# Softmax weights of the first two batches turned in fp32 by TensorE and normalised after P x V

## The reference

```
q, kv  = ln(x), ln(ctx)
qp, kp, vp = q @ Wq.T + bq, kv @ Wk.T + bk, kv @ Wv.T + bv
scores = qh @ kh.T / sqrt(32) - scale[h] * dist(query, key) + offset[h]
attn   = softmax(scores)                  # over the 256 keys
x      = x + (attn @ vh) @ Wo.T + bo
x      = x + gelu(ln(x) @ W1.T + b1) @ W2.T + b2
```

## Time and profile before

| | |
|---|---|
| Runs | 1235.98, 1234.48, 1235.89 us, median 1235.89 |
| Profiled execution | span 1232.5 us from the first to the last instruction; no time of its own around it is given |
| PE | 1203.1 us busy (98%), 9288 products |
| VectorE | 948.1 us busy (77%) |
| ScalarE | 878.1 us busy (71%) |
| GpSimd | 968.8 us busy (79%) |
| Chain that ended last | PE 85%, POOL 4%, DVE 4%, ACT 3%, issue 2% |

### The profile page before, as it was taken

The page is one execution under the profiler, slowest core; times in us unless marked ns, Lnnn a source line. Parts: engine busy times, 40 slices in busy tenths (PEclk is TensorE's granted clock), DMA queues, the critical chain, the costliest instruction groups (busy, mean ns, idle before and its releaser), DMA issues.

```text
span 1232.5 us, 27315 instructions
## 1 busy us (share of the span) xinstructions
PE 1203.1 (98%) x9288; PEld 784.8 (64%) x9288; DVE 948.1 (77%) x2525; ACT 878.1 (71%) x2036; POOL 968.8 (79%) x1191
## 2 busy tenths in 40 slices
PE   8898889999999999999999999999999999999998
PEld 3444466666666666666666666666666666666664
DVE  5899988879897878898787879888787878667321
ACT  7899787777767786777767686777767676676231
POOL 5687989889797879889797878889797878767410
PEclk8999999999999999999999999999999999999999
DMA  8599999988889898988989897998889897787433
GB/s 253 168 236 219 249 211 195 212 195 206 191 199 206 195 218 186 208 205 201 199 190 211 199 220 182 214 201 193 204 189 208 200 212 172 163 180 174 137 118 120
DMA packets 469179, 241.60 MB, mean 196 GB/s; under 512 B 384672, under 2 KB 409392, under 8 KB 469040
## 3 DMA queue, kind: packets, MB, share of 16 engines
q1 hardware_dynamic: 469040, 239.86, 83.7%
HBM read 109.66 MB, written 12.58 MB: 99 GB/s over the span
## 4 chain that ended last, share of the span: by engine, by line
PE 85%; POOL 4%; DVE 4%; ACT 3%; issue 2%; DMA 1%; SPq 1%; DVEq 0%; POOLq 0%; ACTq 0%
PE ps_down L696 27%; PE ps_up L681 27%; PE ps_qk L616 11%; PE ps_vo L640 6%; PE ps_vo L637 6%; PE ps_s L652 4%; PE ps_pv L666 4%; POOL soft L1335 1%; POOL soft L1352 1%; DMA xT<-x_nat 1%; DVE soft L1139 1%; ACT soft L849 1%; DVE p_nat L1157 0%; DVE p_nat L1153 0%; DVE w L1083 0%
## 5 line engine op out<-in xcount | busy, mean ns | idle before, releaser
L681 PE MATMUL ps_up<-hT,w 128*128 128x256 f16 x3072 | 377.2, 273 | 1.6 <-ACT u L895 1.6
L696 PE MATMUL ps_down<-w,hid 128*128 128x512 f16 x1536 | 372.9, 379 | 1.5 <-DMA w<-x_scratch 1.1
L1344 POOL TENSOR_SCALAR p_nat<-soft,row_inv 128x256 f16<-128x256 f32 x468 | 300.2, 652 | 78.9 <-DVE row_inv L1147 78.6
L681 PEld LDWEIGHTS ps_up<-hT,w 128*128 128x128 f16 x3072 | 300.4, 98 | 90.6 <-ACT u L895 1.9
L849 ACT ACTIVATE soft<-soft,neg_max 128x256 f32<-128x256 f32 x512 | 255.3, 500 | 115.7 <-DVE neg_max L1139 114.5
L1139 DVE CUSTOM_DVE_ANT_0 soft<-ps_s,soft,factor 128x256 f32<-128x256 f32 x512 | 225.6, 477 | 126.5 <-PE ps_s L652 126.3
L1157 DVE SCALAR_TENSOR_TENSOR p_nat<-soft,row_inv,p_nat 128x256 f16<-128x256 f32 x468 | 268.1, 612 | 1.9 <-POOL p_nat L1344 1.9
L1352 POOL TENSOR_SCALAR soft<-dist,scale_neg,offset 128x512 f32<-128x512 f32 x256 | 234.2, 915 | 12.6 <-DVE p_nat L1157 10.0
L895 ACT ACTIVATE u<-ps_up,bias,up_scale 128x256 f32<-128x256 f32 x256 | 142.7, 557 | 133.3 <-PE ps_up L681 131.9
L696 PEld LDWEIGHTS ps_down<-w,hid 128*128 128x128 f16 x1536 | 148.6, 97 | 133.2 <-DMA w<-x_scratch 1.8
L1360 POOL TENSOR_SCALAR hid<-u,hid_scale 128x1024 f16<-128x1024 f32 x64 | 81.2, 1268 | 110.6 <-ACT u L901 110.6
(11 more groups left out here) (135 smaller groups left out, 1565.2 us busy)
## 6 DMA issues: line engine op xcount, KB each, us to landing
w<-x_scratch SPq DMA_DIRECT2D x256, 256.0 KB, 3.0
stack<-qk_parts SPq DMA_DIRECT2D x256, 96.0 KB
raw<-in_ctx SPq DMA_DIRECT2D x32, 256.0 KB, 3.8
raw<-in_x SPq DMA_DIRECT2D x32, 256.0 KB, 3.0
c_stage<-in_w SPq DMA_DIRECT2D x16, 512.0 KB, 4.7
x<-in_x SPq DMA_DIRECT2D x32, 256.0 KB, 4.2
out<-x SPq DMA_DIRECT2D x32, 256.0 KB, 3.3
tok_rows<-in_tok_xy SPq DMA_DIRECT2D x16, 256.0 KB, 3.9
```

Source lines behind the costliest of these rows:

```text
L681: mm = e.matmul(ps_up[s % 2][:, 0:L], w_1_sb[:, wp, k, m * P:(m + 1) * P], hT[:, b % 2, :, xp * KT + k, :], start=(k, wp, xp) == (0, 0, 0) ...
L696: mm = e.matmul(ps_down[tt][:], hid[:, chunk % HID_RING, i, hp, tt * P:(tt + 1) * P], w_2_sb[:, s % W2_RING, wp, :], start=(m == 0 and (hp ...
L1344: mine = e.tensor_scalar(p_nat[:, nat, HI, lc, :], soft[:, ring, lc, :], row_inv[:, ring, lc:lc + 1], 1.0, ALU.mult, ALU.mult)
```

## The change

For items 0 to 31 (batches 0 and 1, `FIRST` = 32) the weights stay unnormalised fp32 and are not split.

- ScalarE's `exps` has no row sum; `scaled_sums`, `inverse`, `p_normalise`, `p_hi`, `p_hi_odd`, `p_lo` and `p_turn` are not done for these items.
- PE's `turn(i)`, in slot i + 3 right behind the scores: four fp32 transposes of 128x128, with `soft` as the stationary operand and an identity as the moving one, into `ps_down[i % 2]`. ScalarE's `whole(i)`, in slot i + 4 before `exps`, copies the bank of 512 columns into `pT_whole`, which lies where `pT` lies.
- The values of batches 0 and 1 are kept in fp32 (`v_whole`), one copy of ScalarE and no `v_lo`.
- PE's `attend_whole(G)`, in slot 9 + 4G: eight fp32 products of 256 columns for P x V into `ps_pv[:, 0:256]`, and eight with a stationary of ones for the row sums into `ps_pv[:, 256:512]`.
- VectorE's `attn_whole(G)`, in slot 10 + 4G behind `score_max`: a reciprocal of 128x256 from PSUM into `attn_n`, and a product of 128x256. ScalarE's `attn_hi` and VectorE's `attn_lo` then read `attn_n`.
- `keep_busy` counts two steps for a turn and eight for a group in place of three, writes to `ps_down`, and waits for `whole(slot - 4)`. The output bias is formed in `ps_pv` in place of `ps_down[0]`.
- GpSimd builds the identity (a memset and an `affine_select` of 128x128) before its first slot; `bias_tile` waits for `s_turn` where it waited for `s_plo`.

The core of the diff, each hunk where the functions above are:

```diff
+pT_whole = sb("pT_whole", [P, PT_RING, TC, L], F32, at["pT"])
+v_whole = sb("v_whole", [P, 2, TC, D], F32, at["v_parts"])
+ident = sb("ident", [P, P], F32, at["p_nat"] + (NAT_RING - 1) * 2 * LC * T * 2)
...
-ALL, FIRST = 20, 32
...
+FIRST = 2 * H
+FIRST_HG = FIRST // HPG
+FIRST_TILES = 2 * LC
+SPLIT = N_ITEMS - FIRST
...
-        for i in due(slot, 4, ITEM, N_ITEMS):
-            p_turn(i)
+        for i in due(slot, 4 + FIRST, ITEM, SPLIT):
+            p_turn(FIRST + i)
...
+    def turn(i):
+        ring = i % SOFT_RING
+        gate.wait_ge(s_id, ID_EYE)
+        gate.wait_ge(s_row, ROW_V)
+        gate.wait_ge(s_exp, 2 * i + 2)
+        gate.wait_ge(s_whole, i - 1)
+        for tc in range(TC):
+            for lc in range(LC):
+                at_col = tc * L + lc * P
+                mm = e.transpose(ps_down[i % 2][:, at_col:at_col + P], soft[:, ring, lc, tc * P:(tc + 1) * P], ident[:])
+        mm.then_inc(s_turn)
+
+    def attend_whole(G):
+        b, hg = divmod(G, HG)
+        gate.wait_ge(s_whole, HPG * G + HPG)
+        gate.wait_ge(s_vhi, n_half(b, 1))
+        gate.wait_ge(s_bo_all, 1)
+        gate.wait_ge(s_an, G)
+        for tc in range(TC):
+            for j in range(HPG):
+                h = hg * HPG + j
+                e.matmul(ps_pv[32 * j:32 * j + 32, 0:L], v_whole[:, b, tc, h * HD:(h + 1) * HD],
+                         pT_whole[:, (4 * G + j) % PT_RING, tc, :], start=(tc == 0), stop=(tc == TC - 1))
+        for tc in range(TC):
+            for j in range(HPG):
+                mm = e.matmul(ps_pv[32 * j:32 * j + 32, L:2 * L], one[:].to_broadcast([P, HD]),
+                              pT_whole[:, (4 * G + j) % PT_RING, tc, :], start=(tc == 0), stop=(tc == TC - 1))
+        mm.then_inc(s_pv)
...
+        for i in due(slot, 3, ITEM, FIRST):
+            turn(i)
...
-            taken = 1 + (3 if due(slot, 9, GROUP, N_HG) else 0) + (6 if slot % 2 else 0) + (6 if slot >= UP else 0)
+            taken = 1 + (2 if due(slot, 3, ITEM, FIRST) else 0) + (8 if due(slot, 9, GROUP, N_HG) else 0) + (6 if slot % 2 else 0) + (6 if slot >= UP else 0)
             taken += vo_done + (4 if due(slot, 1, ITEM, MT) else 0)
             taken += 16 if slot == 4 else 0
-            keep_busy(ps_pv if slot < 9 else ps_down[0], max(0, SLOT_STEPS - taken))
+            if slot < 2:
+                keep_busy(ps_pv, max(0, SLOT_STEPS - taken))
+            else:
+                gate.wait_ge(s_row, ROW_V)
+                gate.wait_ge(s_whole, min(slot - 3, FIRST))
+                keep_busy(ps_down[slot % 2], max(0, SLOT_STEPS - taken))
...
+        if b < 2:
+            e.activation(v_whole[:, b, tt, :], ps_vo[:], ACT.Copy).then_inc(s_vhi)
+            return
...
+        if i < FIRST:
+            for lc in range(LC):
+                gate.wait_ge(s_max, 2 * i + lc + 1)
+                e.activation(soft[:, ring, lc, :], soft[:, ring, lc, :], ACT.Exp, scale=-1.0,
+                             bias=neg_max[:, ring, lc:lc + 1]).then_inc(s_exp)
+            return
...
+    def whole(i):
+        gate.wait_ge(s_turn, i + 1)
+        gate.wait_ge(s_pv, (i - PT_RING) // 4 + 1)
+        e.activation(pT_whole[:, i % PT_RING, :, :].rearrange("p c l -> p (c l)"), ps_down[i % 2][:], ACT.Copy).then_inc(s_whole)
...
+        gate.wait_ge(s_o, n_half(b - 2, 1))
+        if G < FIRST_HG:
+            gate.wait_ge(s_an, G + 1)
+            e.activation(attnT[:, b % 2, HI, hg, :], attn_n[:], ACT.Copy).then_inc(s_ahi)
+            return
...
-        for i in due(slot, 3, ITEM, N_ITEMS):
-            if by_scalar(i):
-                p_hi_odd(i)
+        for i in due(slot, 4, ITEM, FIRST):
+            whole(i)
...
+    def attn_whole(G):
+        gate.wait_ge(s_pv, G + 1)
+        gate.wait_ge(s_alo, G)
+        e.reciprocal(attn_n[:], ps_pv[:, L:2 * L]).then_inc(s_recip)
+        gate.wait_ge(s_recip, G + 1)
+        e.tensor_tensor(attn_n[:], ps_pv[:, 0:L], attn_n[:], ALU.mult).then_inc(s_an)
...
+            e.tensor_tensor(attnT[:, b % 2, LO, hg, :], attn_n[:], attnT[:, b % 2, HI, hg, :], ALU.subtract).then_inc(s_alo)
...
             score_max(i)
-        for k in due(slot, 2, 2, N_ITEMS // 2):
-            inverse(k)
+        for k in due(slot, 2 + FIRST, 2, SPLIT // 2):
+            inverse(FIRST // 2 + k)
+        for G in due(slot, 10, GROUP, FIRST_HG):
+            attn_whole(G)
...
+            p_lo(FIRST + i)
...
-        gate.wait_ge(s_plo, i - SOFT_RING + 1)
+        gate.wait_ge(s_turn, min(i - SOFT_RING + 1, FIRST))
+        gate.wait_ge(s_plo, n_split(i - SOFT_RING))
...
+    e.memset(ident[:], 1.0).then_inc(s_id)
+    gate.wait_ge(s_id, ID_EYE - 1)
+    e.affine_select(ident[:], ident[:], pattern=[[-1, P]], compare_op=ALU.is_equal, fill=0.0, base=0, channel_multiplier=1).then_inc(s_id)
...
+            p_hi(FIRST + i)
```

More of the change, by code:

```diff
@@ L120, in build_block @@
         bias_1 = sb("bias_1", [P, MT], F32)
+        attn_n = sb("attn_n", [P, L], F32)
         b_o_sb = sb("b_o", [P, D], F32)
@@ L186, in build_block, with n_split, n_pair_split @@
         N_CHUNKS = MT // CH
-        ALL, FIRST = 20, 32
[L191 to L200, removed]
+        FIRST = 2 * H
+        FIRST_HG = FIRST // HPG
+        FIRST_TILES = 2 * LC
+        SPLIT = N_ITEMS - FIRST
+        def n_split(i):
+            return i - FIRST + 1
+        def n_pair_split(k):
+            return k - FIRST // 2 + 1
         UP = 31
@@ L292, in vo_empty @@
             kind, b, n = vo_before[use]
-            return {"v": (s_vlo, n_half(b, n)), "o": (s_x1, n_half(b, n))}[kind]
+            if kind == "o":
+                return s_x1, n_half(b, n)
+            return v_ready(b, n)
         x_rows = x.rearrange("b (c p) d -> (b c) p d", p=P)
@@ L575, in value_bias_out @@
                 for k in range(KT):
-                    mm = e.matmul(ps_down[0][:], bias_v[:, k, :], w_stage[SEC_O][:, k, :], start=(k == 0), stop=(k == KT - 1))
+                    mm = e.matmul(ps_pv[:], bias_v[:, k, :], w_stage[SEC_O][:, k, :], start=(k == 0), stop=(k == KT - 1))
                 mm.then_inc(s_brow_o)
@@ L1062, in bias_out @@
                 gate.wait_ge(s_bo, DMA)
-                e.tensor_tensor(b_o_sb[:], ps_down[0][:], b_o_sb[:], ALU.add).then_inc(s_bo_all)
+                e.tensor_tensor(b_o_sb[:], ps_pv[:], b_o_sb[:], ALU.add).then_inc(s_bo_all)
             def bias1_columns():
@@ L1241, in vector_program @@
                         mlp_out(2 * b + tt)
-                for i in due(slot, 3, ITEM, N_ITEMS):
-                    if not by_scalar(i):
-                        p_lo(i)
+                for i in due(slot, 3 + FIRST, ITEM, SPLIT):
+                    p_lo(FIRST + i)
                 for which in range(2):
@@ L1277, in vector_program @@
                     for b in due(slot, V_PROJ[tt] + 2, BATCH, B):
-                        v_lo(b, tt)
+                        if b >= 2:
+                            v_lo(b, tt)
         def gpsimd_program(engine):
@@ L1400, in gpsimd_program @@
                     bias_tile(i)
-                for i in due(slot, 2, ITEM, N_ITEMS):
-                    if by_scalar(i):
-                        p_normalise(i)
-                    else:
-                        p_hi(i)
+                for i in due(slot, 2 + FIRST, ITEM, SPLIT):
+                    p_hi(FIRST + i)
                 for w in range(AT_W1, N_W):
```

58 lines of the change are left out of this document (24 added, 34 removed).

## The result

| | before | after |
|---|---|---|
| median (range), 4 runs each | 1235.93 (1234.48 to 1238.63) us | 1250.24 (1249.44 to 1253.47) us |
| ratio, 95% interval | | 1.0122 [1.011, 1.0135], slower |
| profiled execution, span | 1232.5 us | 1251.7 us |
| start of slot 9 / 31 / 37 on PE | 74.56 / 159.61 / 183.85 us | 75.12 / 176.25 / 203.16 us |

The change costs 14.3 us; 1256 was forecast, within 1238 to 1280. The profiled execution of after is the slowest of its four runs (the spans of the other three are 1247.7 to 1248.5), so the two traces differ by 19.2 us, some 3 of which are its own.

What follows compares the result with a forecast made beforehand. PE and VectorE hold each other before slot 37, PE sets the pace after; +15.5 us (slots 9 to 31), +3 (slot 34), +1.5 (slot 37), 0 (slots 2 to 8) make +20, span 1252.5, timed 1256 us, range 1238 to 1280.

Steps and rivals of the forecast that it cites:

- Five pairs of slots between go by PE, 6.92: Slots 11 and 12 and the like: PE sets the pace, 3.23 + 3.69 = 6.92 us each, 34.6 together.
- Product end 4.9 / 5.3 / 4.0: PE's start of slot 9+4G to the products' end: 4.9 us; 5.3 in slots 17, 21, 25; 4.0 in 29.
- The rest of VectorE's slot 2.6: VectorE's other work in slots 10+4G after the pair, less what is removed: 2.6 us for all six.
- A group of fp32 products 1.9: PE's P x V group, 16 products of 256 columns with four column groups side by side: 1.9 us.
- Case C: PE pays more: fp32 halves hold up the next column group or turns cost 0.88 us; 1270 us, chance 10%.
- Reciprocal 2.1: VectorE's 128x256 reciprocal, once per group: 2.1 us, extrapolated from the medians of one and four columns.
- Six times slots 9 and 10: Slots 9 and 10 of six groups, 2 x 10.95 + 3 x 11.35 + 10.05 us: 66.0 together.
- Slots 31 to 37 +3: Slot 34: ScalarE's `attn_hi` waits for the pair, 2.55 and 1.06 us more product time, less slack: +3 us.
- PE's waits for `neg_max`: Sign: `ps_s` waits grow from 11.8 to over 20 us, one of 2 to 3 us every fourth slot.
- Case B: The clock falls in PE's new pauses, +3 us for each of up to seven groups: 1277 us, chance 20%.
- D: The reciprocal on VectorE is cheap, 0.41 us, 13.6 us less: 1242 us, 1235 to 1248, chance 13%.
- E: The chain fits: cheap reciprocal, products and turns; six groups win 3.6 us, nothing added later: 1232 us, chance 12%.

Runs made afterwards that it cites:

- e12: e8 with `attn_whole` again right behind `score_max`; late `attn_hi`/`attn_lo` and nine places kept: 1249.09 us, 1.0104 to before.
- e8: After with `attn_whole` late in slot 10+4G, nine `pT_whole` places, `attn_hi`/`attn_lo` one slot later (except each batch's last group): 1233.54 us, 0.9982 to before.
- e1: After with `attn_whole` moved, until slot 31, to the end of VectorE's slot 10+4G, just ahead of `attn_lo`: 1243.83 us, 1.0072 to before.
- e4: After with 11 more `keep_busy` steps in slots 10, 14, 18, 22, 26 and 30, filling PE's pauses: 1252.02 us, 1.0139 to before.
- e3: After with the 128x256 reciprocal replaced by a `tensor_scalar` writing a constant, normalisation left out: 1244.52 us, 1.0077 to before.
- e10: e8 without the eight products with ones per group, division by row sums left out: 1232.17 us, 0.9965 to before.
- e5: Before plus, in slots 10+4G, VectorE's wait for the group's products and an unread 128x256 reciprocal from SBUF: 1244.20 us, 1.0063 to before.
- e6: After with nine places for `pT_whole` instead of six, so ScalarE's `whole` never waits for the products: 1252.40 us, 1.0132 to before.

## Why the prediction was right

**The place, shown.** The forecast put the whole loss at VectorE's queue behind the wait for the products. e12 against e8 shows it, and slot 10's timeline has each step of it. That the size agrees too (15.5 forecast against before, 15.5 and 15.4 measured against e8) is luck: e8, with the longer products and without the stands, happens to take as long as before in these slots (85.09 and 85.05), and 2.9 of the 15.4 are the clock. What the prediction did not have is that undoing this alone gives back only 6.4 (e1). It looked at VectorE's queue only. ScalarE, with its stands at the copy and at `attn_hi` and its table loads of 1.28 us, was late with `qk_hi`, and `qk_lo`'s stand for it (12.4 us already in after) was waiting behind the first. "Five pairs of slots between go by PE, 6.92" failed there: slots 11 and 12 take 8.07 us in e1.

**The terms.**

- Product end 4.9 / 5.3 / 4.0: measured 4.74, 5.22 and 3.94. The rest of VectorE's slot 2.6: in slot 10 from 82.12 to 84.92, 2.80.
- A group of fp32 products 1.9: from 115.51 to 117.37, 1.86. Turns 0.44: the next operation starts 0.43 us later. Case C is refuted by both.
- Reciprocal 2.1: it takes 1.76. The multiply 0.42. The pair with its step is 2.13 (79.99 to 82.12) for 2.55.
- `score_max` and the step to PE 0.9: from 84.92 to 85.96, 1.04.
- Six times slots 9 and 10, 66.0 forecast: 10.83, 10.40, 10.97, 11.25, 10.77 and 7.61, together 61.8. The last is where a step failed. From slot 31 the scores stand behind `attend`, so PE opens slot 31 with `mlp_up` and does not wait for `score_max(30)`; I had charged it 10.05.
- Five pairs between, 34.6 forecast: 7.35, 8.43, 7.66, 8.33 and 7.51, together 39.3. Of the 4.7 over, 3.3 are the clock in slots 15 and 23 (4.87 and 4.93 for 3.26). The rest are short waits of PE in slots 12, 20 and 28: for `half_out` of the late ScalarE (0.20 and 0.38 us) and for `neg_max` (0.44 and 0.71). The two errors, -4.2 and +4.7, cancel: 101.1 against 100.6. The stretch was right to 0.5 us, by some luck.
- Slots 31 to 37 +3, measured +2.7; slot 37 to 41 +1.5, measured +0.9.
- Slots 2 to 9 0, measured -0.9: slots 2 and 3 are 1.7 us shorter (1 forecast), slots 4 and 5 0.9 longer (0.9 forecast).

With +16.1 for slots 9 to 31 these make +18.8. The traces differ by 19.2 (+20 forecast): after's slot 2 starts 1.5 us later, and what follows slot 41 is 1.0 shorter. Neither was forecast. The late start is mostly that run's own: slot 2 starts at 46.33 us in it, and at 44.59 to 45.67 in the variants. I then added the 3.4 us between before's profiled span and its median to get 1256; after's median lies 1.5 under its profiled span, and these 4.9 make most of the 5.8 us between 1256 and 1250.24.

**The signs.** One named sign failed: PE's waits for `neg_max` were to grow to over 20 us, and they are 13.4. They did turn into few long ones (five of 2.27 to 2.69 us), but there are five and not six, for the reason given at slot 31. The reciprocal lies under its 2.0 to 2.2. The others came: VectorE stands up to 4.0 us before the reciprocal, the group takes 1.86 us, four turns 0.43, and slot 37 starts at 203.16.

**Case B in part.** Of two pauses of over 2 us in the timeline of PE above, after that of 2.69 us twelve projection products still take 1.47, after that of 2.27 us they take 2.38, and the window has a mean clock of 0.61, between full and the 1.2 GHz level. From 194 to 196 us it is 0.50, which the prediction named as the sign of B. There were three such falls, in slots 15, 23 and 34/35; those in slots 15 and 23 cost 1.6 and 1.7 us, where 3 each was forecast. e4 removes two and gains nothing. The turns alone bring no fall: e8 has all of them and a clock of 1.00 from 80 to 205 us. How many falls after's other runs had is not known; they have no trace.

**Cases D and E.** D's pair (0.42 + 0.42) ran as e3: 1244.5, where I had 1242. E needed a reciprocal of 0.41 us and short products too, and at 1.76 and 1.86 us neither is short. Its side, not slower, is reached by another way: e8's order, in which ScalarE still stands for the pair (10.7 us), but `score_max` and PE hardly do.

**Where VectorE's relief went.** The prediction held that only PE's pauses could be won. In slots 9 to 31 PE's own pace before is 11 pairs of 6.92, 76.1 us, so 8.9 of the 85.05 were waits. In e8 the waits are nearly gone, but PE has 1.1 to 1.5 us more per group (slot 9 takes 4.74 for 3.65, slot 17 5.22 for 3.69), some 7.5 for six: 83.6, and 85.09 is measured. So what the relief could give was spent on fp32 products. e10 shows that the next bound is close beneath: with some 5.2 us less on PE in this stretch (slot 9 takes 3.88 for 4.74) only 1.5 came back, as VectorE's own slots with the pair then bound.

GpSimd's and the DMAs' relief was counted at nothing. That fits (with GpSimd 44 us less busy no kernel here is over 0.35% faster than before), but no run took it alone.

## What to carry to other kernels

An operation that waits for another engine belongs behind everything in its queue that does not depend on it; put at the head it costs each group the stand and its own length, and more on an engine that was just relieved, because that engine now comes early. When such a wait is moved, look at once for the next engine that hands over (here ScalarE's half in front of the other's): one stand hides the next. Two of the three moves, tried alone, look worth little (6.4 us and nothing); all three together are worth 16.7. Work taken from an engine beside the bound is worth no more than the waits that it causes; read that sum first, and lay the bound's own new work against it.

## What the runs showed of the hardware

- A reciprocal of 128x256 fp32 takes 1.758 us from PSUM in after, and 1.72 from SBUF in e5. From the 0.173 us of four columns that is (1758 - 173) / 252 = 6.3 ns per further column, under the 7.3 between one column and four. The Trainium skill, "VectorE: DVE Perf Modes", "First, the fixed hardware budget", with its repeat count of 8 gave an estimated 2.1 us; the measurement is 0.37 shorter, so the rule has the order of size and not the number.
- fp32 products on four column groups run side by side as f16 ones do: 16 products of 256 columns with 32 output rows take 1.86 us with both halves (after, from 115.51 to 117.37), where one by one, at 0.95 / 2 each, they would take 7.6.
- Four fp32 transposes of 128x128 take 0.43 us of PE's stream (after, from 86.18 to 86.61), 0.11 each, where an f16 product of 512 columns takes 0.22.
- The length of a pause of PE does not tell whether the clock falls after it. In after, those of 2.27 and 2.62 us (slots 14 and 22) were followed by a fall, those of 2.69, 2.35 and 2.35 us (slots 10, 18 and 26) were not. In e6 the pause of 2.69 us in slot 10 was (clock 0.62 from 84.80 to 88.80), and that of 2.27 in slot 14 was not.
- Before and after each square root of a distance tile ScalarE's trace has a table load of 1.28 us (81.89 and 84.31 us in e1).
